# Two decoder-style cross-attention blocks: one attention unit's probabilities in each layer's first step go through TensorE instead of VectorE and DRAM, with other PSUM banks

## The reference, cut to what matters

```python
def _cross_attention(q_in, kv_in, wq, bq, wk, bk, wv, bv, wo, bo, bias_k, bias_v):
    qh = (q_in @ wq + bq).reshape(b, q_len, H, K)
    kh = (kv_in @ wk + bk).reshape(b, t, H, K)
    vh = (kv_in @ wv + bv).reshape(b, t, H, K)
    # one learned key and value row, bias_k and bias_v, is appended for every head
    logits = einsum('bqhk,bthk->bhqt', qh, kh) / sqrt(K)
    weights = softmax(logits, axis=-1)
    ctx = einsum('bhqt,bthk->bqhk', weights, vh)
    return ctx @ wo + bo

x = x + _cross_attention(layer_norm(x), ctx_2048, ...)   # layer 0
x = x + _cross_attention(layer_norm(x), ctx_2048, ...)   # layer 1
x = x + gelu(layer_norm(x) @ w_fc1 + b_fc1) @ w_fc2 + b_fc2
```

## Time and profile before

| what | value |
|---|---|
| median of 3 runs | 514.39 us (511.93 to 514.67) |
| the profiled execution, its own time | 511.24 us |
| its span from first to last instruction | 509.4 us |
| PE busy | 490.2 us, 96% |
| DVE, ACT, POOL busy | 399.5, 332.4, 409.8 us |
| chain that ended last, PE's share | 85% |
| granted TensorE clock | 1.000 |

### The profile page before, as it was taken

One profiled execution on the slowest core, in us unless ns is written; L12 is line 12 of the kernel. 1 busy time (PEld: TensorE's weight loads), 2 busy tenths in 40 slices (PEclk: granted clock), 3 DMA queues, 4 the chain that ended last, 5 costly groups with the idle time before them and its releaser, 6 DMA issues.

```text
span 509.4 us, 10955 instructions
## 1 busy us (share of the span) xinstructions
PE 490.2 (96%) x3215; PEld 442.2 (87%) x3215; DVE 399.5 (78%) x918; ACT 332.4 (65%) x723; POOL 409.8 (80%) x374
## 2 busy tenths in 40 slices
PE   8898999999999999999888999999999999999887
PEld 6687898999999899999766999989989899999787
DVE  4798887887878878766799878788788788765893
ACT  3677766677767767575367767767676667676431
POOL 3877998989898988896675998989989898987620
PEclk9999999999999999999999999999999999999999
DMA  8338775656666675701308766676767566620101
GB/s 280 129 134 254 234 220 185 194 196 197 181 206 185 206 225 166 228 5 61 103 16 266 243 197 179 200 221 192 219 185 213 190 193 195 196 64 2 42 0 43
DMA packets 54181, 84.66 MB, mean 166 GB/s; under 512 B 6010, under 2 KB 34830, under 8 KB 54158
## 3 DMA queue, kind: packets, MB, share of 16 engines
q1 hardware_dynamic: 54158, 84.38, 54.1%
HBM read 54.47 MB, written 29.88 MB: 166 GB/s over the span
## 4 chain that ended last, share of the span: by engine, by line
PE 85%; DVE 8%; POOL 2%; issue 1%; DMA 1%; ACT 1%; SPq 0%; DVEq 0%; POOLq 0%
PE ring L1116 63%; PE ps_ctx L1116 10%; PE acc L1116 10%; DVE z_sb L880 1%; DMA x_sb<-x_in 1%; PE ring L1156 1%; DVE k_lo L775 1%; DVE blocks L814 1%; DVE bn L869 1%; DVE h_lo L900 1%; DVE h_full L891 1%; POOL wq_lo L334 1%; DVE k_hi L1102 1%; DVE x_sb L861 0%; DVE pT_lo L827 0%
## 5 line engine op out<-in xcount | busy, mean ns | idle before, releaser
L842 DVE TENSOR_REDUCE row_max<-ring 128x1 f32<-128x512 f32 x112 | 76.6, 690 | 32.1 <-PE ring L1116 31.9
L587 ACT ACTIVATE probs<-ring,shift 128x512 f32<-128x512 f32 x112 | 76.4, 682 | 18.9 <-DVE shift L847 18.7
L387 POOL TENSOR_TENSOR v_lo<-v_sum,v_hi 128x512 fp32r<-128x512 f32 x64 | 83.0, 1298 | 6.9 <-ACT v_hi L545 6.9
L394 POOL TENSOR_SCALAR probs<-probs,inv 128x512 f32<-128x512 f32 x80 | 55.8, 703 | 29.2 <-DVE inv L855 29.2
L814 DVE STREAM_TRANSPOSE blocks<-probs 128x512 f32<-128x512 f32 x112 | 72.6, 687 | 0.4
L399 POOL TENSOR_TENSOR pT_lo<-wf_lo,pT_hi 128x1024 fp32r<-128x1024 f32 x28 | 67.1, 2419 | 0.0
L1116 PE MATMUL ring<-pT_lo,v_hi 128*128 128x256 f32 x208 | 58.4, 281 | 0.7 <-DVE pT_lo L827 0.7
L527 ACT ACTIVATE k_hi<-ring,cols 128x512 fp32r<-128x512 f32 x55 | 36.3, 690 | 34.8 <-PE ring L1116 34.6
L1116 PE MATMUL ring<-pT_hi,v_lo 128*128 128x256 f32 x208 | 58.0, 279 | 0.0
L1116 PE MATMUL ring<-pT_hi,v_hi 128*128 128x256 f32 x208 | 58.0, 279 | 0.0
L1116 PE MATMUL ring<-wv_lo,cT_hi 128*128 128x256 f32 x196 | 54.8, 280 | 1.9 <-POOL wv_lo L334 1.9
(11 more groups left out here) (185 smaller groups left out, 1639.7 us busy)
## 6 DMA issues: line engine op xcount, KB each, us to landing
spill<-blocks SPq DMA_DIRECT2D x56, 512.0 KB, 2.9
wf_hi<-spill SPq DMA_DIRECT2D x112, 128.0 KB, 3.2
wf_lo<-spill SPq DMA_DIRECT2D x112, 128.0 KB, 3.3
wk_raw<-wk_in SPq DMA_DIRECT2D x17, 256.0 KB, 2.7
wq_raw<-wq_in SPq DMA_DIRECT2D x17, 256.0 KB, 3.7
wv_raw<-wv_in SPq DMA_DIRECT2D x16, 256.0 KB, 3.8
vrows<-vrows_in SPq DMA_DIRECT2D x16, 256.0 KB, 4.2
wo_raw<-wo_in SPq DMA_DIRECT2D x16, 256.0 KB, 2.7
```

Of the source, the lines that this page charges most:

```text
L387: pool.tensor_tensor(v_lo[:, 2 * m:2 * m + 2, :], v_sum[:, m % 2, :].rearrange("p (t c) -> p t c", c=PW), v_hi[:, 2 * m:2 * m + 2, :].bitc ...
L394: pool.tensor_scalar(probs[:, u, q, :], probs[:, u, q, :], inv[:, u, q:q + 1], 0.0, ALU.mult, ALU.add).then_inc(p_ready_pool, 1)
L587: act.activation(probs[:, u, q, :], ring[S_BANKS[where][QTB * u + q]][:], ACT.Exp, bias=shift[:, u, q:q + 1], scale=SCALE, accum_out=row_s ...
L842: dve.reduce_max(row_max[:, u, q:q + 1], ring[S_BANKS[where][QTB * u + q]][:], AX_X).then_inc(max_done, 1)
```

## The change

In a layer's first step, unit 0's probabilities are transposed by PE (`transpose_first`, eight 128 x 128 transposes into banks 1 and 5, right behind `scores(3, 1)`), rounded by ACT (`round_first`) and split by DVE (`split_first`), in two halves. DVE's two block transposes, SP's write and four reads, ACT's `round_moved` and DVE's `moved_rest` of unit 0 are gone there; SP raises by hand the counts that they would have raised. The tiles made after that point (`project_q` 0 and 1, `project_v` 3, `project_k` 0 to 3) lie in other banks, with other waits, and unit 3's block transposition stands behind all four `split_k` on DVE. In `step`, `scores(0, 0)` now waits for all four value sums of the step before instead of three, and the waits for `k_split` 2 and for `exp_done` 7 of the pair before are gone.

```diff
-V_BANKS = {"first": [None, None, 3, 2], "step": [5, 4, 0, 2], "last": [5, 0, 1, 3], "prologue": [3, 5], "between": [3, 0]}
-K_BANKS = {"first": [5, 2, 3, 5], "step": [1, 3, 1, 3], "last": [2, 2, 1, 5], "prologue": [5, 4, 0, 1]}
+V_BANKS = {"first": [None, None, 3, 0], "step": [5, 4, 0, 2], "last": [5, 0, 1, 3], "prologue": [3, 5], "between": [3, 0]}
+K_BANKS = {"first": [4, 1, 5, 3], "step": [1, 3, 1, 3], "last": [2, 2, 1, 5], "prologue": [5, 4, 0, 1]}
 FIRST_Q_BANKS = [2, 4]
-Q_BANKS = {"first": [1, 0], "step": [3, 4]}
+Q_BANKS = {"first": [2, 3], "step": [3, 4]}
+FIRST_PT_BANKS = [1, 5]
...
# SP, step
+                if first:
+                    if layer > 0:
+                        sp.wait_ge(blocks_ready, NU * (pair - layer))
+                        sp.wait_ge(landed[0], QB * LOAD * (pair - layer))
+                    sp.sem_inc(blocks_ready, 1)
+                    sp.sem_inc(landed[0], QB * LOAD)
+                    sp.sem_inc(spilled[0], LOAD)
...
                 for half in range(2):
-                    for u in (2 * half, 2 * half + 1):
+                    units = [u for u in (2 * half, 2 * half + 1) if u > 0 or not first]
+                    for u in units:
                         write_blocks(pair, layer, u, first)
-                    for u in (2 * half, 2 * half + 1):
+                    for u in units:
                         read_blocks(pair, layer, u, first)
...
# ACT
+            def round_first(pair, layer, q):
+                act.wait_ge(first_filled, QTB * layer + q + 1)
+                if layer > 0:
+                    act.wait_ge(o_filled, NU * (pair - 1) + 3)
+                act.activation(own_tile(pT_hi, 0, q), ring[FIRST_PT_BANKS[q]][:].rearrange("p (n r) -> p n r", r=BLK),
+                               ACT.Copy).then_inc(pT_rounded if q == QTB - 1 else first_rounded, 1)
...
                 exponential(pair, 3, 1, "first", layer, first=True)
+                round_first(pair, layer, 0)
+                round_first(pair, layer, 1)
                 round_q(pair + 1, 1, "first", layer)
...
                 round_k(pair + 1, 2, "first")
-                round_moved(pair, layer, 0, first=True)
                 round_k(pair + 1, 3, "first")
...
# DVE, first_step
                 maximum(pair, 2, 1, "first")
-                transpose_blocks(pair, layer, 0, first=True)
                 shifts(pair, 2, 1)
...
                 inverse_sums(pair, 2)
+                split_q(pair + 1, 0, "first", layer)
                 sum_v(pair, 3, "first")
-                split_q(pair + 1, 0, "first", layer)
+                split_first(pair, layer, 0)
                 inverse_sums(pair, 3)
+                split_first(pair, layer, 1)
                 split_q(pair + 1, 1, "first", layer)
                 transpose_blocks(pair, layer, 2, first=True)
                 split_k(pair + 1, 0, "first")
-                transpose_blocks(pair, layer, 3, first=True)
                 split_k(pair + 1, 1, "first")
-                moved_rest(pair, layer, 0)
                 split_k(pair + 1, 2, "first")
                 split_k(pair + 1, 3, "first")
+                transpose_blocks(pair, layer, 3, first=True)
...
# PE, first_step
+                pe.wait_ge(p_ready_pool, NORMS_POOL * pair + 1)
+                transpose_first(0, layer)
+                pe.wait_ge(p_ready_pool, NORMS_POOL * pair + 2)
+                pe.wait_ge(exp_done, NS * pair + 4)
+                transpose_first(1, layer)
                 pe.wait_ge(wq_split, pair + 2)
+                pe.wait_ge(exp_done, NS * pair + 5)
                 project_q(0, "first")
-                pe.wait_ge(exp_done, NS * pair + 5)
+                pe.wait_ge(exp_done, NS * pair + 6)
                 project_v(3, "first")
+                pe.wait_ge(exp_done, NS * pair + 7)
                 project_k(0, "first")
-                pe.wait_ge(exp_done, NS * pair + 6)
+                pe.wait_ge(exp_done, NS * (pair + 1))
                 project_q(1, "first")
-                pe.wait_ge(v_summed, NV * (pair + 1))
+                pe.wait_ge(first_split, layer + 1)
                 project_k(1, "first")
-                pe.wait_ge(exp_done, NS * (pair + 1))
+                pe.wait_ge(pT_split[0], pair - layer + 1)
                 project_k(2, "first")
-                pe.wait_ge(k_split, NK * (pair + 1) + 1)
+                pe.wait_ge(q_split, NQ * (pair + layer + 3))
                 project_k(3, "first")
...
# PE, step
-                pe.wait_ge(q_split, NQ * (pair + layer + 2))
-                pe.wait_ge(v_summed, NV * (pair - 1) + 3)
+                pe.wait_ge(q_split, NQ * (pair + layer + 1) + 1)
+                pe.wait_ge(v_summed, NV * pair)
                 scores(0, 0, "step")
```

More of the change, by code:

```diff
@@ L187, in build_program @@
         pT_rounded, pT_split = sem("pT_rounded"), [sem(f"pT_split{u}") for u in range(NU)]
+        first_filled, first_rounded, first_split = (sem(f"first_{n}") for n in ("filled", "rounded", "split"))
         own_filled, own_rounded, own_split = sem("own_filled"), sem("own_rounded"), sem("own_split")
@@ L806, in transpose_blocks @@
                         dve.wait_ge(spilled[u + 2], LOAD * done)
-                else:
+                elif not first or u == 3:
                     dve.wait_ge(spilled[u - 2], LOAD * (done + 1))
+                elif layer > 0:
+                    dve.wait_ge(spilled[u], LOAD * done)
+                if first and u == 1:
+                    dve.wait_ge(spilled[0], LOAD * (done + 1))
                 if ACT_TILES[u]:
@@ L822, in moved_rest, with split_first @@
                                   pT_hi[:, u % 2, :, :].bitcast(F32).rearrange("p c (i q) -> p c i q", i=QB), ALU.subtract).then_inc(pT_split[u], 1)
+            def split_first(pair, layer, q):
+                if q < QTB - 1:
+                    dve.wait_ge(first_rounded, layer + 1)
+                else:
+                    dve.wait_ge(pT_rounded, NU * (pair - layer) + 1)
+                dve.tensor_tensor(own_tile(pT_lo, 0, q), ring[FIRST_PT_BANKS[q]][:].rearrange("p (n r) -> p n r", r=BLK),
+                                  own_tile(pT_hi, 0, q).bitcast(F32), ALU.subtract).then_inc(pT_split[0] if q == QTB - 1 else first_split, 1)
             def split_own(pair, layer, j):
@@ L1150, in scores, with transpose_first @@
                 product(ring[S_BANKS[where][QTB * u + q]][:], [(*tile, k_hi[:, h, part], k_lo[:, h, part])]).then_inc(s_filled, 1)
+            def transpose_first(q, layer):
+                for t in range(CTB):
+                    last = pe.transpose(ring[FIRST_PT_BANKS[q]][:, t * P:(t + 1) * P], probs[:, 0, q, t * P:(t + 1) * P], ident[:])
+                last.then_inc(first_filled, 1)
             def transpose_own(j):
@@ L1283, in step @@
                 scores(0, 1, "step")
+                pe.wait_ge(v_split, NV * (pair - 1) + 2)
                 pe.wait_ge(pT_split[0], done)
-                pe.wait_ge(k_split, NK * pair + 2)
-                pe.wait_ge(v_split, NV * (pair - 1) + 2)
                 context(0, "step")
@@ L1289, in step @@
                 scores(1, 0, "step")
-                pe.wait_ge(exp_done, NS * (pair - 1) + 7)
                 scores(1, 1, "step")
```

## The result

Over 16 runs of each, the changed kernel has a median of 515.02 us (513.63 to 517.31) and the kernel before 512.85 us; the ratio over the single runs is 1.0050, 95% interval 1.0035 to 1.0066 (the quotient of the two medians is 1.0042). One run of the kernel before, of 2758.65 us, stands apart and is left out of the ratio. The forecast was 514.8, range 510.6 to 516.6, no change within 0.5%; measured is a loss of 0.35 to 0.66%, at the edge of what can be told. The profiled execution took 513.82 us with a span of 512.0, against 511.24 and 509.4.

The account below looks back on a forecast made before the run. The prediction took PE, busy 96% of the span, as the bound. The exchanged waits came to +0.4 us at a landing of 3.3, so 511.24 became 511.6, plus 3.15 of level 514.8; range 510.6 to 516.6.

Parts of the forecast that it names:

- The transposes: On PE, eight added transposes in each layer's first step, put at 0.83 us from overlapping rows.
- The old waits: PE's stops ahead of project_k(3), 0.66 us, and the second scores, 1.28 us, both for DVE's k_lo, would go.
- the prediction's walk along the rows: Layer 1 on PE: last key matmul at 275.58, second scores at 276.50, 2.1 us earlier than before.
- The wait that appears: PE's project_q(0) waits for ACT's exponential behind round_moved(2), held by unit 2's late reads: 1.5 to 2.5 us idle.
- The sum for both layers: Later project_q(0) in layers 1 and 0 plus long first matmuls: 0.1 + 0.46 + 0.2 = +0.76 us.
- The level: Median of three runs of the kernel before stands 3.15 us above its profiled execution; added to the forecast.
- each new stop also costs the 0.1 us of a first matmul: On PE, the first matmul after each new stop is 0.1 us longer, 0.2 us in all.
- No gain was left standing: Rival: both PE stalls go and nothing replaces them, 3.8 us less, 510.6; chance 0.16.
- No stall appeared inside the first step: Rival: project_k(1) and (2) wait for split_first, DVE 1.5 us late, 517.8; chance 0.06.
- The transposes did overlap: Rival: PE's eight transposes don't overlap, 2.8 us instead of 0.83, +4.4 in all, 518.8; chance 0.03.
- The slow landing: Rival: unit 2's fourth read behind the write lands after 4.6 us, one issue takes 1.45, +5.0, 519.4; chance 0.08.
- 0.96 us of cover in one layer: In layer 0, the wait for DRAM ahead of round_moved(2) lay hidden behind PE by 0.96 us.

Follow-up runs that it names:

- the filler: Seven idle matmuls of zeros in PE's prologue gap before the first project_v, added to the changed kernel: 513.04 us against 512.16 for the kernel before, ratio 1.0017.

## Why the prediction was right, and by how much its sizes were off

**The transposes.** 0.83 us forecast, 0.79 measured in each layer. The estimate of 2.2 us from the Trainium skill, "TensorE: Matmul & The Clock Gate", Part 4, does not hold in this stream, and the clock stayed full around both groups.

**The old waits.** Gone, as forecast. The last key matmul starts at 277.45 and the second scores at 278.46. Shifted by the 1.85 us that the first trace had gained up to the first transpose (267.19 against 265.34), the prediction's walk along the rows said 277.43 and 278.35.

**The wait that appears.** Its place, its cause and its size are as forecast. DVE, then ACT, layer 1:

```profile
278.61 0.75 DVE L795 SCALAR_TENSOR_TENSOR k_lo<-ring,cols,k_hi 128x512 fp32r<-128x512 f32 x1 [0.21 <-ACT k_hi L538]
...
279.28 1.29 DVE L838 STREAM_TRANSPOSE blocks<-probs 128x512 f32<-128x512 f32 x2
```

```profile
277.89 0.69 ACT L538 ACTIVATE k_hi<-ring,cols 128x512 fp32r<-128x512 f32 x1 [0.47 <-PE ring L1149]
...
286.95 1.06 ACT L573 ACTIVATE pT_hi<-wf_lo 128x1024 fp32r<-128x1024 f32 x1 [3.12 <-DMA wf_lo<-spill]
...
288.48 0.19 ACT L606 ACTIVATION_READ_ACCUMULATOR probs<-ring,shift 128x1 f32 x1
```

From the key matmul 0.44 to ACT, 0.72 to DVE, transposes done at 280.57; the walk said 278.7 + 1.85. Then SP, and the write of unit 3 with the four reads of unit 2:

```profile
276.54 0.34 SPq L255 DMA_DIRECT2D spill<-blocks  x1
...
281.18 1.12 SPq L265 DMA_DIRECT2D wf_lo<-spill  x2
```

```profile
L265 SPq DMA_DIRECT2D wf_lo<-spill x4: 318/458/762, 281.2 to 282.9; - x4
...
L255 SPq DMA_DIRECT2D spill<-blocks x1: 337/337/337, 280.7 to 280.7; - x1
...
DMA to landing us min/median/max: 3.0/3.2/4.1
```

The write starts at 280.7, the fourth read at 282.9, and ACT's `round_moved(2)` at 286.95: 6.25 us from write to use where I took 5.5 to 5.7. The slowest of the reads lands 4.1 us after its issue, against 3.3 taken and 3.5 seen in the steady step. That is the only term of this chain that was too small, 0.6 us in layer 1 of this trace; in layer 0 it was 5.7, as taken. From `round_moved` to PE it was 1.78 against 1.79. The sum for both layers was +0.76 at a landing of 3.5 and +0.4 at 3.3. Less the 0.2 of the two long first matmuls, which the path doesn't hold, that is +0.56 and +0.2, where the path measured +1.16, +1.16 and +0.40 us in three traces. As time between runs at full clock it is 512.29 - 511.65 = +0.64 and 512.10 - 511.58 = +0.52, but only three runs of the changed kernel are at full clock, two and one.

**The number is luck in part.** For the edit itself the forecast was +0.4 us; between the medians it is 515.02 - 512.85 = +2.17. The level, 3.15 us above the profiled execution, came from three runs; over 16 it is 512.85 - 511.24 = 1.61. So the edit was put 1.8 us too low and the level 1.5 too high, and 514.8 comes within 0.2 us of the measured median because the two nearly cancel.

**What the sum left out.** The other 1.6 us between the medians. The step that failed is "each new stop also costs the 0.1 us of a first matmul": a stop of 2 us can cost more, because the clock may be granted at half level behind it. The runs split by clock in all three sessions, and a low run costs about 1.2 to 1.5 us more in the kernel before and 2.4 to 3.8 in the changed one. There some runs have two low stretches by their mean clock (those at 0.993 lie near 516), but its runs at 0.997 also cost 2.3 and, in one case, 2.65 us more. The table of paths says where part of that may lie: the two traces with a low prologue have a path of +1.16, the three without one +0.22 to +0.40. Why the landing is slower in them isn't shown, and so a comparison at full clock may leave out a part of what the edit costs. The changed kernel had 30 low runs of 33, the kernel before 21 of 66. Where it happens in the prologue, seen beside a trace in which it doesn't: PE's rows (the second is four transposes), then the clock, of the changed kernel and of the one with SP's order mended.

```profile
16.50 0.39 PE L1149 MATMUL ring<-wv_lo,cT_hi 128*128 128x256 f32 x1 [1.98 <-POOL wv_lo L345]
...
17.99 1.01 PE L1232 MATMUL ring<-ident,z_sb 128*128 128x128 f32 x4
```

```profile
18.00:21.40 3.40, 3.40 (x18) 0.51 0.83 275
```

```profile
16.58 0.38 PE L1154 MATMUL ring<-wv_lo,cT_hi 128*128 128x256 f32 x1 [1.99 <-POOL wv_lo L350]
...
18.06 0.60 PE L1237 MATMUL ring<-ident,z_sb 128*128 128x128 f32 x4
```

```profile
18.00:21.40 3.40, 3.29 (x28) 1.00 0.86 266
```

The gap of 1.98 and 1.99 us is the same; in one the clock falls to 0.51 behind it and in the other it does not. The four transposes are not the cause: in the changed kernel's second trace the clock falls at 17.7, ahead of them (18.36). Filling this gap removed low runs in all three kernels without a long second stop (0 of 28 in all; without the filler 28 of 95 in before and the versions with a short or no stop at `project_q(0)`). With the filler the changed kernel kept 8 of 22. So two places with chances of about 0.3 and 0.4 are shown. Together they would make 0.55 of the runs low; that it was 30 of 33, and that two of its three traces had the low stretch in a prologue which the edit doesn't touch, is not explained and stays open. With the same prologue and SP's order mended, 1 run of 11 was low.

**The rivals.** No gain was left standing, as DRAM's landing did bind. No stall appeared inside the first step: `split_first` was in time. The transposes did overlap. The slow landing went a third of the way to its own rival in layer 1 of the first trace.

## What to carry to other kernels

When a wait on the bound engine is removed, walk on to the next thing that waits for a long chain and price it from the same row as before: here a DRAM round trip with 0.96 us of cover in one layer lost all of it, since the same edit started the trip later. Read the order of the DMA queue as part of the chain; the mend was to read unit 2 before writing unit 3, and it turned a loss of 0.5% into a gain of 0.5%. Where runs have different mean clocks, compare runs of equal clock first, and then ask which stops of the engine lie ahead of the low stretches. And price the change against the kernel before, not only the new median: here the median was met while the change was missed by 1.8 us.

## What the runs showed of the hardware

The clock fell to half level behind stops of TensorE of 1.8 to 2.0 us in an otherwise full stream, in some executions and not in others of the same program; in each of the five traces that have such a stretch it began 0.9 to 1.5 us behind the stop's end and lasted 3.4 us. Stops of 1.8 to 2.4 us passed without it too (1.84 and 2.40 at `project_q(0)` in the first trace of the changed kernel), as did the 1.6 us at the start of layer 1. Where the stop at `project_q(0)` was 1.2 us in the trace and the prologue's was filled, none of 10 runs was low. Unit 2's reads in layer 1, right behind unit 3's 512 KB write in the same queue, landed after 3.0 to 4.1 us; issued ahead of that write they landed after 2.5 to 2.9 us. The two traces differ in other traffic too.
